# First attention of a two-layer vision transformer: closing steps and weight splits at other bursts, and the guard's branch between two scores

## The chip, the cores and the metric

The kernel is one program on one core of a Trainium2 chip. The metric is device time in microseconds (us), the median of several executions. The engines are PE (TensorE, matrix products), VectorE (DVE), ScalarE (ACT), GpSimd (POOL) and SyncE (SP, which issues DMAs); each works its own instruction list in order, and semaphores tie them together.

## The reference

Eight images of 32 x 32 tokens pass a tokeniser and two layers, each of attention and a mixture of experts. The part that the change touches is the first attention, with softmax over 1024 keys in 8 heads of 16, and its closing:

```python
h = tok(x)                                # (8, 1024, 128)
xn = layernorm(h)
Q, K, V = (xn @ Wq.T + bq, xn @ Wk.T + bk, xn @ Wv.T + bv)   # 8 heads of 16
attn = softmax(Q K^T / 4);  context = attn V
out = context @ Wo.T + bo + xn
out = (out - mean) / sqrt(var + 1e-5) * gamma + beta
h = h + out                               # first residual
h = h + moe_0(layernorm(h), ...)          # 2 of 8 experts for an image
h = h + attn_1(layernorm(h), ...);  h = h + moe_1(layernorm(h), ...)   # 2 of 8 for a token
```

(In the reference the layer's heads come from a plain reshape, so each head of an image holds 128 tokens' worth of rows, spread over the eight column groups.)

## The kernel before

`embed_and_attend` does the first attention. A **batch** is one image; there are eight. A batch has 64 **units**: four head pairs (HP) of 16 units. For a unit PE makes scores (`scores`, L826) of 128 keys against 512 queries for both heads of the pair into one of three psS buffers, ScalarE takes the exponential of all 128 x 1024 (L741) into one of four probs buffers, and PE multiplies them by the values into psO (`weigh`, L838). Two units are a **burst**; a batch has 32 bursts, numbered m, and eight of them make a pair. In burst m PE waits for the exponential of unit 2m + 1, issues the scores of units 2m + 3 and 2m + 4, at a pair's first burst the projection of an earlier pair (`project`, L391), then `weigh` for units 2m and 2m + 1, and then a step of the next batch's embedding.

At a **pair change** (between bursts 7 and 8, 15 and 16, 23 and 24, 31 and 0) VectorE must transpose psO out (`out_of_psum`, L1015, in the last burst of a pair) before PE may begin the next pair's first value product. After it come `add_input` (L397), which frees psA for PE's next step, and `divide` (L1019 to L1025).

Between these, three kinds of work hang on the burst numbers.

- **Steps of the next batch** (`STEPS`): E embeds, T transposes, q and k project, N takes norms for the guard, v projects; each for two halves (0, 1). VectorE reads each result (`embed_read`) and works it on (`embed_rest`); GpSimd squares q and k (L671). N waits on PE for the square of k of its half.
- **Closing steps** (`finish`), for half 0 and half 1 of a batch's tokens: add_bias (L435, then moments), normal (L105), moments, second (L105, L448), score (L450, L452). GpSimd has a part in three of them: a root (L402) after add_bias and after moments, and after normal the **stream** (L410, L412, L414), which updates the residual and which moments waits for. `UPPER` holds those done in the batch after, `LOWER` those in the same batch. The order of the table sets VectorE's and GpSimd's order alike.
- **Weight splits** (`SPLIT`): VectorE splits one raw expert weight tile in two (L1031, L1033), GpSimd stores the result (L710) and loads the next raw tile (L705). A split waits for its tile's load and for the store before.

The **guard** bounds the scores. At burst 24 VectorE branches on the flag `unsafe` (`guard`), and on PE `rescue` (L812) reads the same flag at burst 25; with this input neither branch is entered. `drain` on an engine waits until its earlier writes are done.

The last batch (`more` false) has no steps of a next one; it has the gating of the experts (`GATES`, `POOLED`, `PE_TILES`) and its own splits.

## Time and profile before

| | |
|---|---|
| median of 3 runs | 1405.86 us (1405.33 to 1407.46) |
| profiled execution | 1408.95 us |
| its span in the trace | 1407.1 us |
| PE busy | 1187.5 us (84%) |
| ScalarE busy | 995.0 us (71%) |
| VectorE busy | 934.7 us (66%) |
| GpSimd busy | 564.4 us (40%) |
| first attention, first to last exponential | from 56.6 to 624.5 us |

The busy shares are means over four stages with different limits. What matters here is the first 630 us, and in them which engine waits for which. A wait in square brackets at the end of a timeline row is the engine's idle time just before it.

### The profile page before, as it was taken

Reading aid. Unit: us, or ns where it says so; the run is one execution under the profiler, and the core shown is the slowest. Engines: PE = TensorE matmul, PEld = TensorE weight load, DVE = VectorE, ACT = ScalarE, POOL = GpSimd, SP = SyncE. Lnnn points to the kernel's source line nnn. Section 1 sums busy time; section 2 is a strip of 40 time slices with the busy share of each in tenths; the row PEclk is TensorE's granted clock in tenths of the full one; section 3 lists DMA queues with packets and bytes.
Section 4 is the critical chain, followed back from the end, with each engine's and each line's share of the span. In section 5 each row is a group of like instructions: output and inputs, shape, how many; then the busy total and the mean of one; then the engine's idle time right before and its main releaser. Section 6 shows DMA issues by size and latency. Waiting matters only on the chain. (4 is left out here: it accounts for less than half of the span.)

```text
span 1407.1 us, 26982 instructions
## 1 busy us (share of the span) xinstructions
PE 1187.5 (84%) x9386; PEld 795.1 (57%) x9386; DVE 934.7 (66%) x2612; ACT 995.0 (71%) x1348; POOL 564.4 (40%) x546
## 2 busy tenths in 40 slices
PE   3599999999999999889989996888872899999940
PEld 2244444444444444447768874777762688888830
DVE  4255868686868686758978884677662466666625
ACT  0288888888888888858868984454520799999930
POOL 3413333333333333210201000077777177777660
PEclk9599999999999999979999997889875899999975
DMA  3655565555555555223211300011115577777609
GB/s 86 119 129 146 120 157 130 147 130 148 139 138 137 138 135 139 84 71 124 88 61 61 119 2 8 1 49 47 50 47 174 181 242 237 241 245 244 234 24 358
DMA packets 93163, 180.57 MB, mean 128 GB/s; under 512 B 15597, under 2 KB 64200, under 8 KB 84960
## 3 DMA queue, kind: packets, MB, share of 16 engines
q1 hardware_dynamic: 72832, 129.18, 32.8%
q0 software_dynamic: 17344, 42.68, 9.4%
q10 hardware_dynamic: 2848, 6.95, 1.7%
q8 instruction: 76, 1.25, 0.4%
q14 instruction: 63, 0.52, 0.1%
HBM read 116.96 MB, written 63.12 MB: 128 GB/s over the span
## 5 line engine op out<-in xcount | busy, mean ns | idle before, releaser
L741 ACT ACTIVATE a_probs<-a_psS 128x1024 f32<-128x1024 f32 x512 | 484.0, 1034 | 91.5 <-PE a_psS L826 58.2
L838 PE MATMUL a_psO<-a_probs,a_v 128*32 128x256 f32 x4096 | 282.1, 394 | 17.3 <-DVE a_o_t L1015 16.9
L1252 DVE TENSOR_TENSOR f_g_lo<-f_g,f_g_hi 128x512 fp32r<-128x512 f32 x284 | 195.1, 689 | 121.1 <-ACT f_g L1159 120.1
L2044 POOL DMA_INDIRECT result<-f_out,f_idx x156 | 182.7, 1171 | 92.5 <-issue 61.0
L838 PEld LDWEIGHTS a_psO<-a_probs,a_v 128*32 128x32 f32 x4096 | 108.5, 111 | 154.0 <-issue 88.9
L1636 POOL DMA_INDIRECT queue<-all_row,all_idx x128 | 126.0, 984 | 38.5 <-issue 37.8
L826 PE MATMUL a_psS<-ag_qs,ag_ks 50*128 50x512 f32 x512 | 97.4, 457 | 15.7 <-DMA ag_qs<-a_gparts 8.5
L826 PE MATMUL a_psS<-a_qs,a_ks 50*128 50x512 f32 x512 | 96.8, 454 | 7.8 <-issue 3.4
L402 POOL TENSOR_TENSOR ag_rs_f<-ag_veps_f,all_half 128x4 f32<-128x4 f32 x32 | 34.1, 1066 | 124.4 <-DVE ag_veps_f L99 124.4
L1422 POOL TENSOR_TENSOR ah_rs<-ah_veps,all_half 128x4 f32<-128x4 f32 x16 | 18.5, 1156 | 154.3 <-DVE ah_veps L1435 154.2
L826 PEld LDWEIGHTS a_psS<-ag_qs,ag_ks 50*128 50x128 f32 x512 | 39.9, 191 | 63.4 <-issue 31.6
L826 PEld LDWEIGHTS a_psS<-a_qs,a_ks 50*128 50x128 f32 x512 | 39.3, 189 | 54.7 <-ACT a_probs L741 37.5
L1166 ACT ACTIVATE f_x_hi<-f_psX 128x512 fp32r<-128x512 f32 x55 | 33.1, 602 | 43.2 <-PE f_psX L1191 43.2
L710 POOL DMA_DIRECT2D experts<-a_split x32 | 19.7, 615 | 108.6 <-DVE a_split L1033 108.6
L1156 ACT ACTIVATE f_g_hi<-f_psH,all_w 128x512 fp32r<-128x512 f32 x76 | 53.1, 699 | 10.1 <-PE f_psH L72 9.5
L1156 ACT ACTIVATE f_g_hi<-f_psH,ag_qs 128x512 fp32r<-128x512 f32 x72 | 50.3, 699 | 12.3 <-PE f_psH L72 11.6
L1156 ACT ACTIVATE f_g_hi<-f_psH,f_w 128x512 fp32r<-128x512 f32 x64 | 44.6, 697 | 18.9 <-PE f_psH L72 17.9
L1156 ACT ACTIVATE f_g_hi<-f_psH,ag_ks 128x512 fp32r<-128x512 f32 x72 | 51.0, 708 | 7.9 <-PE f_psH L72 7.5
L1159 ACT ACTIVATE f_g<-f_psH,all_w 128x512 f32<-128x512 f32 x76 | 53.1, 699 | 0.0
L1159 ACT ACTIVATE f_g<-f_psH,ag_ks 128x512 f32<-128x512 f32 x72 | 51.0, 709 | 0.0
L1159 ACT ACTIVATE f_g<-f_psH,ag_qs 128x512 f32<-128x512 f32 x72 | 50.3, 699 | 0.0
L1191 PE MATMUL f_psX<-all_ident,all_rows 128*128 128x128 f32 x156 | 24.4, 281 | 28.7 <-DMA all_rows<-queue 26.3
(368 smaller groups left out, 2878.8 us busy)
## 6 DMA issues: line engine op xcount, KB each, us to landing
all_w<-experts SPq DMA_DIRECT2D x19, 1026.5 KB, 5.5
experts<-a_split POOLq DMA_DIRECT2D x32, 512.0 KB, 4.8
ag_qs<-experts SPq DMA_DIRECT2D x14, 1026.5 KB, 5.3
ag_ks<-experts SPq DMA_DIRECT2D x14, 1026.5 KB, 5.2
all_rows<-queue SPq DMA_DIRECT2D x39, 260.0 KB, 5.1
f_w<-experts SPq DMA_DIRECT2D x8, 1026.5 KB, 5.5
qparts<-a_parts SPq DMA_DIRECT2D x16, 512.0 KB, 4.5
kparts<-a_parts SPq DMA_DIRECT2D x14, 512.0 KB, 3.1
```

The lines of the kernel that those rows point to most:

```text
L402: self.nc.gpsimd.tensor_tensor(self.rs_f[:, :], self.veps_f[:, :], half[:, 0:TPC], ALU.pow).then_inc(self.root_f, 1)
L710: pool.dma_start(experts[stage][e, :, 2 * layer * HID:2 * (layer + 1) * HID], split[:, :, :].rearrange("p a h -> p (a h)").bitcast(F32)).t ...
L741: nc.scalar.activation(probs[u % NPR][:, :], psS[score_buffer(u)][:, :, :].rearrange("p a n -> p (a n)"), ACT.Exp).then_inc(exp_done, 1)
L826: last = nc.tensor.matmul(psS[score_buffer(u)][:, p, :], ks[par][64 * p:64 * p + KG, kt, hp * P:(hp + 1) * P], queries(par, hp, p, a), sta ...
L838: last = nc.tensor.matmul(psO[32 * g:32 * g + 32, a * HALF:(a + 1) * HALF], v[par][:, 2 * hp + p, kt, :], probs[u % NPR][:, cols:cols + HA ...
L1156: nc.scalar.activation(g_hi[i][:, n, :], psH[n][:, :], ACT.Gelu, bias=bias(m, n))
L1159: nc.scalar.activation(g[:, n, :], psH[n][:, :], ACT.Gelu, bias=bias(m, n)).then_inc(g_done, 1)
L1166: nc.scalar.activation(x_hi[j % 2][:, :], psX[:, :], ACT.Copy).then_inc(hi_done, 1)
L1191: last = nc.tensor.transpose(psX[:, i * P:(i + 1) * P], rows(m)[:, i, 0:D], ident[:, :])
L1252: nc.vector.tensor_tensor(g_lo[i][:, n, :], g[:, n, :], g_hi[i][:, n, :].bitcast(F32), ALU.subtract).then_inc(lo_done, 1)
L1636: pool.indirect_dma_start(queue, bass.IndirectOffsetOnAxis(ap=idx[n % NROW][:, k, t:t + 1], axis=0), row[n % NROW][:, k, t, :], None).then ...
L2044: pool.indirect_dma_start(result, bass.IndirectOffsetOnAxis(ap=idx[i][:, j:j + 1], axis=0), out[i][:, j, :], None, bounds_check=2 * B * S ...
```

## The change

It changes numbers in three tables and one position in PE's code.

- Splits of batches 0 to 6 go from bursts 7, 15, 22, 27 to 10, 14, 22, 28.
- Of the closing steps, moments 0 goes from burst 2 of the next batch to burst 30 of the same (`LOWER`, and for the last batch, which `KEEP` leaves out, it stays where it was, behind this phase). Second 0 goes from 4 to 2, score 0 from 6 to 4, add_bias 1 from 10 to 15, normal 1 from 12 to 18, moments 1 from 18 to 20, score 1 from 25 to 26, add_bias 0 from 26 to 25, normal 0 from 28 to 27. Second 1 stays at 23.
- `rescue` on PE stands between the scores of units 53 and 54 instead of ahead of both. Its spare score buffer is then one (`FREE`), not two, which changes only code inside the branch.

```diff
-    SPLIT = [{7: 0, 15: 1, 22: 2, 27: 3}] * (B - 1) + [{5: 0, 12: 1, 16: 2, 21: 3}]
+    SPLIT = [{10: 0, 14: 1, 22: 2, 28: 3}] * (B - 1) + [{5: 0, 12: 1, 16: 2, 21: 3}]
...
-    FREE = (score_buffer(2 * RESCUE), score_buffer(2 * RESCUE + 1))
-    UPPER = {2: ("moments", 0), 4: ("second", 0), 6: ("score", 0), 10: ("add_bias", 1), 12: ("normal", 1), 18: ("moments", 1), 23: ("second", 1),
-             25: ("score", 1)}
-    LOWER = {26: ("add_bias", 0), 28: ("normal", 0)}
+    FREE = score_buffer(2 * RESCUE + 4)
+    UPPER = {2: ("second", 0), 4: ("score", 0), 15: ("add_bias", 1), 18: ("normal", 1), 20: ("moments", 1), 23: ("second", 1), 26: ("score", 1)}
+    LOWER = {25: ("add_bias", 0), 27: ("normal", 0), 30: ("moments", 0)}
+    KEEP = (25, 27)
...
-                    if m in LOWER:
+                    if m in LOWER and (more or m in KEEP):
...
-                    if more and m == RESCUE:
-                        rescue(b + 1, 1 - par, uses.next())
-                        uses.count -= 1
                     for u in (2 * m + 3, 2 * m + 4):
                         if u < UNITS or more:
                             scores(b, par, u)
+                        if more and u == 2 * RESCUE + 3:
+                            rescue(b + 1, 1 - par, uses.next())
+                            uses.count -= 1
```

GpSimd in a steady batch, from the square of q of the first half at burst 9 to the split's store at burst 22, before:

```order
L671 TENSOR_TENSOR a_qsq<-a_qf 128x512
L402 TENSOR_TENSOR ag_rs_f<-ag_veps_f,all_half 128x4
L671 TENSOR_TENSOR a_ksq<-a_kf 128x512
L410 TENSOR_TENSOR ag_res<-ag_res,ag_brow 128x512
L412 TENSOR_TENSOR ag_res<-ag_res,ag_brow 128x512
L414 TENSOR_TENSOR all_H<-all_H,ag_res 128x512
L710 DMA experts<-a_split 128x1024
L705 DMA a_raw<-w 128x512
L671 TENSOR_TENSOR a_qsq<-a_qf 128x512
L402 TENSOR_TENSOR ag_rs_f<-ag_veps_f,all_half 128x4
L671 TENSOR_TENSOR a_ksq<-a_kf 128x512
L710 DMA experts<-a_split 128x1024
```

and with the change, from the same square of q to the second half's square of k at burst 19:

```order
L671 TENSOR_TENSOR a_qsq<-a_qf 128x512
L710 DMA experts<-a_split 128x1024
L705 DMA a_raw<-w 128x4x128
L671 TENSOR_TENSOR a_ksq<-a_kf 128x512
L710 DMA experts<-a_split 128x1024
L705 DMA a_raw<-w 128x512
L402 TENSOR_TENSOR ag_rs_f<-ag_veps_f,all_half 128x4
L671 TENSOR_TENSOR a_qsq<-a_qf 128x512
L410 TENSOR_TENSOR ag_res<-ag_res,ag_brow 128x512
L412 TENSOR_TENSOR ag_res<-ag_res,ag_brow 128x512
L414 TENSOR_TENSOR all_H<-all_H,ag_res 128x512
L671 TENSOR_TENSOR a_ksq<-a_kf 128x512
```

The stream (L410 to L414) stood behind the first half's square of k; now it stands between the second half's squares of q and k.

VectorE in a steady batch around the change at burst 15, from the read of the transposed second half (T 1, burst 13) to the read of q of that half (burst 17), before:

```order
L105 TENSOR_SCALAR ag_res<-ag_res,ag_mv_f,ag_rs_f 128x128 x4
L912 COPY a_nT<-a_psA 128x512
L940 CAST a_nT_hi<-a_nT 128x512
L942 TENSOR_TENSOR a_nT_lo<-a_nT,a_nT_hi 128x512
L1015 STREAM_TRANSPOSE a_o_t<-a_psO 128x512
L1031 CAST a_split<-a_raw 128x512
L1033 TENSOR_TENSOR a_split<-a_raw,a_split 128x512
L397 TENSOR_TENSOR ag_res<-a_psA,ag_n 128x256
```

and with the change:

```order
L912 COPY a_nT<-a_psA 128x512
L940 CAST a_nT_hi<-a_nT 128x512
L942 TENSOR_TENSOR a_nT_lo<-a_nT,a_nT_hi 128x512
L1031 CAST a_split<-a_raw 128x512
L1033 TENSOR_TENSOR a_split<-a_raw,a_split 128x512
L1015 STREAM_TRANSPOSE a_o_t<-a_psO 128x512
L435 TENSOR_TENSOR ag_res<-ag_res,ag_brow 128x512
L94 BN_STATS ag_stat_f<-ag_res 128x6 x4
L97 BN_AGGR ag_mv_f<-ag_stat_f 128x2 x4
L99 TENSOR_SCALAR ag_veps_f<-ag_mv_f 128x4
L397 TENSOR_TENSOR ag_res<-a_psA,ag_n 128x256
```

Normal 1 (L105) is gone from the place in front, the split (L1031, L1033) stands ahead of the transpose instead of behind it, and add_bias 1 (L435 to L99) stands between the transpose and add_input (L397).

PE at burst 25, the first of the places where it stands:

```order
 L391 MATMUL a_psA<-ag_w_raw,ag_ctxT 128x128 x2
 L838 MATMUL a_psO<-a_probs,a_v 32x256 x8
+L826 MATMUL a_psS<-ag_qs,ag_ks 128x512 x2
 L812 TENSOR_LOAD a_unsafe
 L812 ISA x2
```

One of the burst's two scores (two products) now stands ahead of the load of the flag; the other follows the branch.

## Rows read from the trace of the kernel before

**Rows 1.** The page's part 5: line, engine, group, count; busy, mean ns; idle before, by releaser.

```profile
L741 ACT ACTIVATE a_probs<-a_psS 128x1024 f32<-128x1024 f32 x512 | 484.0, 1034 | 91.5 <-PE a_psS L826 58.2
```

**Rows 2.** Timeline of ScalarE, batch 4: start, us, what, count, idle before.

```profile
361.59 2.86 ACT L741 ACTIVATE a_probs<-a_psS 128x1024 f32<-128x1024 f32 x3 [1.66 <-PE a_psO L838]
...
379.46 2.86 ACT L741 ACTIVATE a_probs<-a_psS 128x1024 f32<-128x1024 f32 x3 [1.73 <-PE a_psO L838]
...
397.91 5.61 ACT L741 ACTIVATE a_probs<-a_psS 128x1024 f32<-128x1024 f32 x6 [1.17 <-PE a_psS L826]
...
413.51 2.85 ACT L741 ACTIVATE a_probs<-a_psS 128x1024 f32<-128x1024 f32 x3 [0.29 <-PE a_psO L838]
```

**Rows 3.** Timeline of PE, batch 4.

```profile
357.03 1.07 PE L838 MATMUL a_psO<-a_probs,a_v 128*32 128x256 f32 x16
...
374.82 1.07 PE L838 MATMUL a_psO<-a_probs,a_v 128*32 128x256 f32 x16
...
378.69 1.07 PE L838 MATMUL a_psO<-a_probs,a_v 128*32 128x256 f32 x16 [1.37 <-DVE a_o_t L1015]
...
389.89 0.38 PE L772 MATMUL a_psA<-a_ksq,a_pieces 128*32 128x512 bf16 x1
...
397.37 0.73 PE L826 MATMUL a_psS<-ag_qs,ag_ks 50*128 50x512 f32 x4 [1.34 <-issue]
```

**Rows 4.** Timeline of VectorE, batch 4, bursts 2 to 18.

```profile
351.19 0.87 DVE L94 BATCH_NORM_STATS2 ag_stat_f<-all_H 128x6 f32<-128x128 f32 x4
...
360.07 0.71 DVE L1015 STREAM_TRANSPOSE a_o_t<-a_psO 128x512 f32<-128x512 f32 x1
...
372.62 1.88 DVE L105 TENSOR_SCALAR ag_res<-ag_res,ag_mv_f,ag_rs_f 128x128 f32<-128x128 f32 x4
...
377.94 0.70 DVE L1015 STREAM_TRANSPOSE a_o_t<-a_psO 128x512 f32<-128x512 f32 x1
...
380.11 0.42 DVE L397 TENSOR_TENSOR ag_res<-a_psA,ag_n 128x256 f32<-128x256 f32 x1
...
382.35 0.75 DVE L918 TENSOR_SCALAR a_qf<-a_psA,a_bcol 128x512 f32<-128x512 f32 x1 [0.19 <-PE a_psA L72]
...
384.47 0.87 DVE L94 BATCH_NORM_STATS2 ag_stat_f<-all_H 128x6 f32<-128x128 f32 x4
```

**Rows 5.** Timeline of GpSimd, batch 4, the stream and the squares.

```profile
372.60 1.04 POOL L671 TENSOR_TENSOR a_ksq<-a_kf 128x512 bf16<-128x512 f32 x1 [1.16 <-DVE a_parts L951]
374.58 1.29 POOL L410 TENSOR_TENSOR ag_res<-ag_res,ag_brow 128x512 f32<-128x512 f32 x1 [0.93 <-DVE ag_res L105]
...
377.60 1.53 POOL L414 TENSOR_TENSOR all_H<-all_H,ag_res 128x512 f32<-128x512 f32 x1
...
388.69 1.04 POOL L671 TENSOR_TENSOR a_ksq<-a_kf 128x512 bf16<-128x512 f32 x1 [1.53 <-DVE a_parts L951]
```

**Rows 6.** Timeline of VectorE, batch 4, bursts 26 to 31.

```profile
401.47 0.69 DVE L435 TENSOR_TENSOR ag_res<-ag_res,ag_brow 128x512 f32<-128x512 f32 x1
...
403.91 0.69 DVE L926 TENSOR_TENSOR a_v<-a_psA,ag_brow 128x512 f32<-128x512 f32 x1
...
405.80 1.12 DVE L105 TENSOR_SCALAR ag_res<-ag_res,ag_mv_f,ag_rs_f 128x128 f32<-128x128 f32 x4
...
411.45 0.72 DVE L1015 STREAM_TRANSPOSE a_o_t<-a_psO 128x512 f32<-128x512 f32 x1 [2.67 <-PE a_psO L838]
```

**Rows 7.** Loads of the raw weight tile, 300 to 420 us: issue to landing.

```profile
DMA to landing us min/median/max: 4.4/6.4/11.1
```

**Rows 8.** Timeline of ScalarE in the last batch.

```profile
562.61 0.24 ACT L221 ACTIVATE ag_e_sc<-ag_sc 128x48 f32<-128x48 f32 x1 [1.48 <-DVE ag_sc L281]
...
589.37 2.85 ACT L741 ACTIVATE a_probs<-a_psS 128x1024 f32<-128x1024 f32 x3 [1.88 <-PE a_psO L838]
```

**Rows 9.** Timeline of VectorE in the last batch.

```profile
625.66 1.11 DVE L105 TENSOR_SCALAR ag_res<-ag_res,ag_mv_f,ag_rs_f 128x128 f32<-128x128 f32 x4 [1.15 <-POOL ag_rs_f L402]
```

**Rows 10.** Two us behind a pair change of batch 1: engines' busy time, PEclk, DMA.

```profile
152.00:154.00 2.00, 2.00 (x16) 0.77 (x18) 1.89 (x6) 1.08 (x2) 0.99 (x2) 0.50 0.64 244
```

More of the change, by code:

```diff
@@ L796, in maximum @@
                         rows, cols = slice(64 * p, 64 * p + KQ), slice(hp * P, (hp + 1) * P)
-                        pe.wait_ge(pre_max, j * T + (b * (T * KT) + h + 1))
+                        pe.wait_ge(pre_max, j * T + (b * (T * KT) + h + 2))
                         for a in range(2):
-                            last = nc.tensor.matmul(psS[FREE[h % 2]][:, a, :], stage[rows, cols], ks[par][rows, 4 * a:4 * a + 4, cols],
+                            last = nc.tensor.matmul(psS[FREE][:, a, :], stage[rows, cols], ks[par][rows, 4 * a:4 * a + 4, cols],
                                                     start=True, stop=True)
@@ L981, in maximum @@
                         dve.sem_inc(waited, 1)
-                        nc.vector.tensor_reduce(negmax[:, h % 2, bass.ds(j, 1), h // 2], psS[FREE[h % 2]][:, :, :].rearrange("p a n -> p (a n)"),
+                        nc.vector.tensor_reduce(negmax[:, h % 2, bass.ds(j, 1), h // 2], psS[FREE][:, :, :].rearrange("p a n -> p (a n)"),
                                                 AX, ALU.max, negate=True).then_inc(pre_max, 1)
@@ L1074, in batch @@
                         shared.finish(dve, part, b - 1, half_, H, mean1, rstd1, score1)
-                    if m in LOWER:
+                    if m in LOWER and (more or m in KEEP):
                         part, half_ = LOWER[m]
```

## The prediction

> **What bounds the kernel now.** I read the page's costliest groups first, then the waits of ScalarE, then one steady batch row by row on every engine. The attention phase runs 512 exponentials one behind the other; ScalarE is busy 484.0 us with them and idle 91.5 us in front of them [rows 1]. Only that idle time can be won. All times below are of batch 4, the fifth of eight.
>
> In that batch ScalarE waits 1.66 us at unit 20 and 1.73 us at unit 36, behind the pair changes at bursts 8 and 16, but only 0.29 us behind the one at burst 0 [rows 2]. The first two come from VectorE. At burst 7 the last value product starts at 357.03 and takes 1.07, so it is done at 358.10 [rows 3]; the transpose that empties psO starts at 360.07, 1.97 late, since VectorE is still at earlier steps [rows 4]. At burst 15 the product is done at 374.82 + 1.07 = 375.89 and the transpose starts at 377.94, 2.05 late [rows 3, 4]; PE then stands 1.37 before the new pair's first product [rows 3]. At burst 31 VectorE waits for PE instead (2.67 idle ahead of the transpose at 411.45) [rows 6], and the change costs the 0.29. A transpose 1.97 late costs 1.66 - 0.29 = 1.37, so about 0.6 us of lateness is hidden (by the projection that PE does there). The fourth idle place is the guard's branch: PE idle 1.34, ScalarE 1.17 [rows 2, 3].
>
> **Burst 7.** Moments 0 leaves burst 2. It costs what add_bias costs without its addition: 403.91 - 401.47 - 0.77 = 1.67 us [rows 6]. The score moves from 6 to 4, the split from 7 to 10: order alone. The transpose moves from 360.07 to 358.4, 0.3 late, which is hidden. Gain 1.37.
>
> **Burst 15.** Add_bias 1 and normal 1 leave the bursts in front of it (2.44 and, with its block, 1.88) and two splits of some 1.2 us each come in. GpSimd's three-part update (stream) leaves too; in the old order the transposed tile's split waited it out. VectorE then has time to spare, if the second weight tile is in. The transpose falls to 375.89 - 1.37 = 374.5 and the gain is 1.73 - 0.29 = 1.44. Together 2.81 per batch by burst 17.
>
> **Burst 21, where I expect it to be given back.** In the new order GpSimd does the stream between the squares of q and k of the second half. PE's norm step N 1 at burst 21 waits for the square of k, which so far lay ahead of nothing but a root. The chain, from the transpose at 374.55 on: 0.64 for it, 2.44 for add_bias 1 (now between the transpose and add_input), 382.35 - 380.11 - 0.19 = 2.05 for add_input and division, so q 1 is read at 379.7 [rows 4, 6]. Its parts take 384.47 - 382.35 = 2.12, to 381.8, and GpSimd squares them. Normal 1 goes in beside that square; the same pair lay together at 372.60, and normal 1 took 1.88 there against 1.12 alone [rows 4 to 6]. So it ends at 383.65. The stream took 377.60 + 1.53 - 374.58 = 4.55, so it ends at 388.3, and the square of k, 1.04, at 389.4 [rows 5]. N 1 started at 389.89 before [rows 3]; with the pair changes won it would be due at 389.89 - 2.81 = 387.1, and can now start at 389.5. PE stands 2.4 us, its next scores are late by that, and ScalarE has about nothing in hand here. What is left of 2.81 is 0.4.
>
> Normal 1's time hangs on the block. The Trainium skill (SBUF — State Buffer, on its engine ports) says that VectorE in a two-port mode or with two SBUF inputs and a GpSimd instruction hold the shared port pair exclusively, and the loser waits the whole instruction. By that rule the block returns beside the q square, as the row shows; without it the sum would be 0.76 better per batch.
>
> **Burst 31.** The sum of add_bias 0 and score 1 is what it was, so v 0 is read at 403.91 less some 0.2. Normal 0 now follows at once, to 405.5 (1.12); the stream ends at 410.1, moments 0 can only then run, to 411.8. The transpose stood at 411.45 [rows 6]; it would now be due at about 410.8. It is late by a full us, 0.6 of it hidden. What burst 25 and the remainder of burst 21 won (0.3 + 0.4) is all but gone: the new batch starts 0.1 earlier, measured against the old. The split pushed behind it waits for GpSimd's instructions too; nothing needs it soon.
>
> **The branch.** PE still runs it in line; only one score, 0.33 us of PE, now lies beside it, and ScalarE gets unit 53 on time but waits for unit 54 instead. Worth 0.3 on PE's chain, not 1.17, because the steps v 0 and v 1 behind it keep PE the limit. If nothing of it overlaps it is 0, if ScalarE were the limit it would be 0.9. I take 0.3 (nearest to the row of PE).
>
> **The weight tile.** It is loaded behind the split at burst 10 (old clock 368.4) and wanted by the split at burst 14, from 373.4 on. Landings ran from 4.4 to 11.1, median 6.4 [rows 7]; the 4.4 fell into quiet DMA, as most of this one does. I take 5.2, so 0.2 us late, which delays the whole chain to burst 21. Bounds: 4.4 costs nothing, 6.4 costs 1.4.
>
> So a steady batch ends with -0.1 + 0.2 = +0.1; for batches 1 to 6 that is 0.6. Batch 0 has no closing steps of a batch before; I take 0.
>
> **The last batch** keeps its splits and has no k square, so there the moves are free. (a) ScalarE waits 1.48 at unit 10 for the shift [rows 8]; ahead of the shift moments 0 goes (1.67) and second 0 comes (1.12 for an instruction group like normal 0, and 0.2 for a copy), and the division there no longer meets a stream, whose instructions last 1.3 and block for half of that on average: 1.67 - 1.3 + 0.7 = 1.1. (b) The change at burst 16 costs 1.88 [rows 8]; with add_bias 1 and normal 1 out of the way 1.88 - 0.29 = 1.6. (c) At the end add_bias 0 stands a burst earlier and normal 0 no longer waits for its root, 1.15 before [rows 9]; 0.9 of it reaches the phase's end. Together 3.6.
>
> **The sum.** 3.6 - 0.6 = 3.0 us. The profiled execution took 1408.95; so 1405.95 in it. The runs' median is 1405.86, 3.09 below the profiled one, so 1402.9. A measurement here tells 0.2%, 2.8 us, from no change; 3.0 lies on that edge. Own range of this case: each steady batch by 0.4 either way (2.4 us), the last by 1: 1399.5 to 1406.
>
> **Rivals.**
> - *The square of k is not late* (chance 0.15). If add_bias or the division run sooner or PE has slack at burst 21, the 2.81 stays in part. Each us that N 1 comes earlier is worth 6 us; half of the wait gone gives 1402.9 - 7 = 1396, all of it 1389. For it: the order itself was laid out to free the pair changes, and both transposes have room. Against: four GpSimd instructions stand in line, with rows for each.
> - *The weight tile is late* (0.12, the slower side). At a landing of 6.4 each of six batches loses 1.2 more than I took: 1402.9 + 7 = 1410. It decides from a landing of about 6.2, where the kernel becomes slower by over 0.2%. For it: k's parts are stored and loaded again just then. Against: 4.4 in the same burst range before.
> - *The clock* (0.08). The granted clock was 0.50, that is 1.2 GHz, for 2 us behind the pair change of batch 1 [rows 10], after PE had stood still at it. The new stand at burst 21 is longer. A dip costs about 1.3 (the exponentials come at 1.5 us there instead of 0.94); in four batches more than before 5 us: 1408. With fewer stands at pair changes it may as well fall away.
> - *The last batch gives nothing* (0.15): its gains are eaten by the summing of the pooled tiles, which now runs under the stream and feeds burst 21. Then 1402.9 + 2.5 = 1405.4, no change.
>
> My forecast has 0.5. Its range lies half on either side of 1403.05, the edge, with more on the faster side. Faster: 0.15 + 0.31 + 0.03 = 0.49. Slower: 0.09 of the weight tile, 0.03 of the clock, 0.01 of the rest: 0.13. Same: 0.38. The range leaves out a tenth at each end: the full gain of the first rival below, the late tile above: 1394 to 1409.
>
> **What would show it.** In the trace after: ScalarE's waits at units 20 and 36 at 0.3 in each steady batch; a new wait of some 2 us at unit 47, put down to scores, with N 1 waiting for the square of k; GpSimd's stream between the two squares; the wait at unit 4 grown from 0.29 to 0.7 or so; that at 53 gone and one of about 1 at 54; VectorE waiting for stream_done at burst 30; steady batches still 70 us long. In the last batch the 1.88 and most of the 1.48 gone. I am wrong if unit 47 has no wait, if unit 36 still has one of over 1, or if batches shorten by more than 0.5 us.

## The result, and the profile after

| | before | after |
|---|---|---|
| median of the runs on one chip | 1405.46 us (20 runs) | 1413.8 us (20 runs, 1410.31 to 1419.44) |
| ratio after to before, 95% interval | | 1.006 [1.0045, 1.0074] |
| profiled execution, its span | 1408.95 us, 1407.1 us | 1411.72 us, 1409.9 us |
| start of unit 4, batches 1 and 7 | 132.83 and 555.52 us | 124.19 and 559.79 us |
| a steady batch, a sixth of that | 70.45 us | 72.60 us |
| start of unit 4 of batch 7 to last exponential | 69.0 us | 66.4 us |

The changed kernel is slower by 0.6%, some 8 us; the forecast was 1402.9. In the profiled executions a steady batch is 2.15 us longer instead of 0.1, and the last one 2.6 shorter instead of 3.6. The spans differ by only 2.8 us, because the profiled execution of the kernel before lost time at its start: its first exponential stands at 56.6 instead of 52.1, ahead of everything that the change touches, and from there to unit 4 of batch 1 it took 76.2 us instead of 72.1. (Two other kernels whose batch 0 is that of before, in experiments 3 and 9, took 71.8 and 72.1.)

The answer to [rows 1], the page's part 5: the exponentials are as long as before, and the idle time looks hardly more, 92.1 us against 91.5. That sum hides the loss. Batch 0 has 19.1 us of it before (8.12 in front of the first exponential) and 9.2 after (2.48 there); the six steady batches have 58.6 and 68.8.

```profile
L741 ACT ACTIVATE a_probs<-a_psS 128x1024 f32<-128x1024 f32 x512 | 485.3, 1033 | 92.1 <-PE a_psS L826 64.5
```

Timeline of ScalarE, batch 5 of after, which answers to [rows 2] (units 20, 36, 47, 48, 49, 50, 52 and then unit 4 of the next batch):

```profile
433.22 2.86 ACT L741 ACTIVATE a_probs<-a_psS 128x1024 f32<-128x1024 f32 x3 [0.29 <-PE a_psO L838]
...
449.70 2.86 ACT L741 ACTIVATE a_probs<-a_psS 128x1024 f32<-128x1024 f32 x3 [0.29 <-PE a_psO L838]
...
463.88 1.02 ACT L741 ACTIVATE a_probs<-a_psS 128x1024 f32<-128x1024 f32 x1 [2.81 <-PE a_psS L826]
465.20 1.02 ACT L741 ACTIVATE a_probs<-a_psS 128x1024 f32<-128x1024 f32 x1 [0.29 <-PE a_psO L838]
466.71 1.02 ACT L741 ACTIVATE a_probs<-a_psS 128x1024 f32<-128x1024 f32 x1 [0.48 <-PE a_psS L826]
467.99 1.94 ACT L741 ACTIVATE a_probs<-a_psS 128x1024 f32<-128x1024 f32 x2 [0.26 <-PE a_psO L838]
470.28 6.63 ACT L741 ACTIVATE a_probs<-a_psS 128x1024 f32<-128x1024 f32 x7 [0.36 <-PE a_psO L838]
...
488.11 2.85 ACT L741 ACTIVATE a_probs<-a_psS 128x1024 f32<-128x1024 f32 x3 [1.49 <-PE a_psO L838]
```

Both pair changes are won: 0.29 at units 20 and 36. A wait of 2.81 has come in at unit 47. Three small ones follow it; the exponentials start 1.3 to 1.5 us apart there. And unit 4 waits 1.49 instead of 0.29. The mean over batches 1 to 6 makes a ledger of ScalarE's waits (of 0.15 us and more), in us per batch:

| units | before | after | forecast of the difference |
|---|---|---|---|
| 20 and 36 | 3.31 | 0.58 | -2.81 |
| 47 | 0 | 3.12 | +2.4 |
| 48 to 52 | 0.29 | 1.58 | 0 |
| 53 to 58 | 1.03 | 0 | (-0.3 on PE) |
| 4 | 0.29 | 1.60 | +0.4 |
| others | 4.86 | 4.59 | 0 |
| all | 9.78 | 11.47 | |

The rest of the 2.15 is in no printed wait: exponentials in a row overlap a little (seven take 6.63 above), and one that stands alone takes 1.02.

The chain behind unit 47, in three timelines of the same batch. VectorE (answers to [rows 4]), the transpose of burst 15, add_input, normal 1, and moments 1:

```profile
447.64 0.72 DVE L1015 STREAM_TRANSPOSE a_o_t<-a_psO 128x512 f32<-128x512 f32 x1 [0.27 <-PE a_psO L838]
...
455.04 1.88 DVE L105 TENSOR_SCALAR ag_res<-ag_res,ag_mv_f,ag_rs_f 128x128 f32<-128x128 f32 x4
...
461.91 0.87 DVE L94 BATCH_NORM_STATS2 ag_stat_f<-all_H 128x6 f32<-128x128 f32 x4 [1.80 <-POOL all_H L414]
```

GpSimd (answers to [rows 5]), the stream between the two squares:

```profile
455.02 1.04 POOL L671 TENSOR_TENSOR a_qsq<-a_qf 128x512 bf16<-128x512 f32 x1 [3.12 <-DVE a_parts L951]
456.99 1.29 POOL L410 TENSOR_TENSOR ag_res<-ag_res,ag_brow 128x512 f32<-128x512 f32 x1 [0.93 <-DVE ag_res L105]
458.93 1.55 POOL L412 TENSOR_TENSOR ag_res<-ag_res,ag_brow 128x512 f32<-128x512 f32 x1 [0.65 <-issue]
460.62 1.26 POOL L414 TENSOR_TENSOR all_H<-all_H,ag_res 128x512 f32<-128x512 f32 x1
461.84 1.04 POOL L671 TENSOR_TENSOR a_ksq<-a_kf 128x512 bf16<-128x512 f32 x1
```

PE (answers to [rows 3]), N 1 and the burst behind it:

```profile
463.02 0.38 PE L772 MATMUL a_psA<-a_qsq,a_pieces 128*32 128x512 bf16 x1 [2.69 <-POOL a_ksq L671]
...
464.00 1.93 PE L838 MATMUL a_psO<-a_probs,a_v 128*32 128x256 f32 x16
465.87 1.22 PE L826 MATMUL a_psS<-a_qs,a_ks 50*128 50x512 f32 x4
```

N 1 starts 463.02 - 447.64 = 15.38 us behind the transpose; the forecast's chain has 389.5 - 374.55 = 14.95. PE stands (is idle and waits) for 2.69 us. What the forecast does not have is in the next row: the 16 value products take 1.93 where [rows 3] has 1.07, and the four score products 1.22 instead of 0.73. Windows of 2 us say why; the granted clock is the figure behind the five engines' busy times:

```profile
462.00:464.00 2.00, 0.98 (x6) 0.42 (x6) 1.77 (x11) 0.12 (x1) 1.31 (x2) 1.00 0.88 263
464.00:466.00 2.00, 2.00 (x20) 0.75 (x18) 1.60 (x8) 1.71 (x2) 0.59 (x1) 0.51 1.08 181
466.00:468.00 2.00, 2.00 (x20) 0.83 (x20) 0.81 (x2) 1.26 (x3) 0.81 (x2) 0.63 1.13 168
468.00:470.00 2.00, 2.00 (x28) 1.13 (x24) 1.54 (x5) 1.93 (x2) 0.59 (x1) 1.00 1.15 168
```

After the stand PE works at 0.51, that is 1.2 GHz, for some 3 us, is busy all of that time and still gives ScalarE a tile only every 1.3 to 1.5 us. The answer to [rows 10] is this in every one of the six steady batches; in those of the kernel before, the clock fell in two (at 151 and 519 us).

At burst 31 VectorE's moments 0 waits for the stream, and the transpose is late (its wait for PE in [rows 6] is gone):

```profile
485.02 0.87 DVE L94 BATCH_NORM_STATS2 ag_stat_f<-all_H 128x6 f32<-128x128 f32 x4 [2.05 <-POOL all_H L414]
...
486.58 0.71 DVE L1015 STREAM_TRANSPOSE a_o_t<-a_psO 128x512 f32<-128x512 f32 x1
```

In the last batch the 1.88 of [rows 8] is 0.29, and nothing is left of the 1.48 in front of the exponential of the gating. But PE stands long at the sum of the pooled tiles, half a pair behind, and unit 47 waits 4.61:

```profile
606.76 1.30 PE L246 MATMUL a_psA<-ag_ones,ag_n 128*128 128x1 f32 x8 [3.28 <-DVEq L317]
```

The phase's end, which answers to [rows 9]: ScalarE's first instruction behind the last exponential, before and after.

```profile
633.51 0.60 ACT L1166 ACTIVATE f_x_hi<-f_psX 128x512 fp32r<-128x512 f32 x1 [7.84 <-PE f_psX L1191]
```

```profile
635.41 0.60 ACT L1166 ACTIVATE f_x_hi<-f_psX 128x512 fp32r<-128x512 f32 x1 [8.11 <-issue]
```

The last exponential starts at 624.5 and at 626.2, so that stretch takes 9.0 us before and 9.2 after: nothing is won there.

### The profile page after: what moved, and what is told of

It is laid out like the page before. It is cut to its first block and busy times, and to the rows that moved or that the text cites. A ratio compares the mean times of both kernels' runs of the same rounds, so it can differ in the third digit from the quotient of the medians.

```text
span 1409.9 us, 26982 instructions
## 1 busy us (share of the span) xinstructions
PE 1192.5 (85%) x9386; PEld 796.0 (56%) x9386; DVE 929.1 (66%) x2612; ACT 996.4 (71%) x1348; POOL 565.2 (40%) x546
## 5 line engine op out<-in xcount | busy, mean ns | idle before, releaser
L741 ACT ACTIVATE a_probs<-a_psS 128x1024 f32<-128x1024 f32 x512 | 485.3, 1033 | 92.1 <-PE a_psS L826 64.5
L2044 POOL DMA_INDIRECT result<-f_out,f_idx x156 | 183.1, 1174 | 92.1 <-issue 61.3
L671 POOL TENSOR_TENSOR a_qsq<-a_qf 128x512 bf16<-128x512 f32 x16 | 17.4, 1090 | 102.5 <-DVE a_parts L951 102.5
```

The source lines that it names most:

```text
L741: nc.scalar.activation(probs[u % NPR][:, :], psS[score_buffer(u)][:, :, :].rearrange("p a n -> p (a n)"), ACT.Exp).then_inc(exp_done, 1)
L2044: pool.indirect_dma_start(result, bass.IndirectOffsetOnAxis(ap=idx[i][:, j:j + 1], axis=0), out[i][:, j, :], None, bounds_check=2 * B * S ...
```

## The experiments

Each ratio is to the kernel before on the same chip; kernels are compared with each other by these ratios, since the chips differ. "A batch" is again a sixth of the time from unit 4 of batch 1 to unit 4 of batch 7, in one profiled execution. It scatters by itself: two kernels with the steady batches of before have 70.45 and 71.28 in theirs. In the first the granted clock fell twice in these batches, in the second five times, four of them at pair changes.

### 1. N 1 two bursts later

```diff
-             20: ("N", 0), 21: ("N", 1), 27: ("v", 0), 29: ("v", 1)}
+             20: ("N", 0), 23: ("N", 1), 27: ("v", 0), 29: ("v", 1)}
```

> The changed kernel with one step moved: PE's second norm product, N 1, stands at burst 23 instead of 21, so the square of k has two bursts more. Theory A (the loss is PE's stand of 2.7 us at burst 21, and the half clock that follows it): the wait at unit 47 (2.8 to 3.7 us in batches 1 to 6) and the clock's fall at bursts 22 and 23 (1.5 us a batch) go; of the 4 us some 1.5 come back as a longer wait at burst 31, so 2 to 2.5 us for each of six batches: 12 to 15 us under the changed kernel's 1413.8, a ratio to before of 0.995 to 0.998. Theory B (the loss is at burst 31, moments 0 behind its stream): the wait at unit 47 goes but the one at unit 4 grows by as much, the time stays within 3 us of the changed kernel's, ratio 1.004 to 1.006.

Measured: 1415.01 us, 1.009 [1.0062, 1.0119]; a batch 71.64. The wait at unit 47 is gone, and ones of 1.9 to 3.2 at unit 52 and 0.9 to 3.1 at unit 4 stand in its place; the clock still falls four times in the steady batches. Timeline of PE: the projection at the pair change waits for N 1's result to be read, which VectorE does late.

```profile
468.56 0.71 PE L391 MATMUL a_psA<-ag_w_raw,ag_ctxT 128*128 128x128 f32 x4 [1.49 <-DVE a_norms L921]
```

Neither theory foresaw that. N 1 as such is no cure: the stand has moved.

### 2. Seven products that nobody reads, ahead of N 1's wait

```diff
                 elif kind == "N":
+                    if b and ch:
+                        for i in range(7):
+                            nc.tensor.matmul(ps, wq_lo[:, :], nT_hi[ch][:, :], start=True, stop=True)
                     pe.wait_ge(sq_done, 2 * n)
```

> The changed kernel, with seven products of 512 columns that nothing reads put on PE ahead of N 1's wait for the square of k (2.3 us of work in a stand of 2.7); the result is unchanged. It parts the stand's own length from the clock. If the half clock behind the stand comes from PE's idleness in it, the granted clock stays at full through bursts 22 and 23, and 1.5 us a batch come back: 8 to 9 us under the changed kernel, ratio 1.000. If the clock falls for another reason (DMA, or what the steps are), nothing comes back: ratio 1.005 to 1.007.

Measured: 1402.76 us, 0.9984 [0.9964, 1.0004]; a batch 70.48. The kernel does more and N 1 starts no earlier (15.32 us behind the transpose, 15.38 without the products), yet by the ratios it is 11 us faster than the changed kernel, and the intervals lie apart. Timeline of PE, batch 5, and one window:

```profile
452.82 1.90 PE L772 MATMUL a_psA<-a_nT_hi,a_wq_lo 128*128 128x512 f32 x7
455.52 0.39 PE L775 MATMUL a_psA<-a_qsq,a_pieces 128*32 128x512 bf16 x1 [0.80 <-POOL a_ksq L671]
...
456.51 1.07 PE L841 MATMUL a_psO<-a_probs,a_v 128*32 128x256 f32 x16
```

```profile
456.00:458.00 2.00, 2.00 (x24) 0.86 (x24) 1.60 (x8) 1.61 (x2) 1.02 (x1) 1.00 1.11 166
```

PE's idle time is 0.80 instead of 2.69, the value products take 1.07, and the clock stays at 1.00 in all six steady batches. ScalarE still waits 2.82 at unit 47 (mean of six), but 0 instead of 1.16 at units 48 to 51 and 0.98 instead of 1.60 at unit 4. So the stand by itself gives back what the two pair changes won, and the clock behind it is what makes the change slower than the kernel before. (The products aren't free: in batch 0, where there is no stand to fill, unit 47 now waits 1.86.)

### 3. The branch alone, in the kernel before

```diff
-                    if more and m == RESCUE:
-                        rescue(b + 1, 1 - par, uses.next())
-                        uses.count -= 1
                     for u in (2 * m + 3, 2 * m + 4):
                         if u < UNITS or more:
                             scores(b, par, u)
+                        if more and u == 2 * RESCUE + 3:
+                            rescue(b + 1, 1 - par, uses.next())
+                            uses.count -= 1
```

(with `FREE` as in the change)

> The kernel before with the third part of the change alone: the guard's branch on PE between the two scores of burst 25. By my prediction's term 0.3 us a batch, 2 us in all: ratio 0.9985. By the trace of the changed kernel, where the load of the flag takes 0.30 us instead of 1.1 to 1.2 and PE is idle 0.3 instead of 1.34, some 1 us a batch: 6 to 7 us, ratio 0.995. ScalarE's wait at unit 53 (0.66 to 1.28) gone, at unit 54 under 0.7.

Measured: 1406.11 us, 1.0013 [0.9992, 1.0034]; a batch 70.46, against 70.45. The wait at unit 53 is gone, 0.46 to 1.39 stand at unit 54. No gain shows: the 0.3 a batch would be 0.9985, just outside the interval. Nor did the load of the flag become short by its place: its median is 768 ns here, 870 in the kernel before and 304 in the changed one.

### 4. Moments 0 at burst 0 of the next batch, in the changed kernel

```diff
-    UPPER = {2: ("second", 0), ...
-    LOWER = {25: ("add_bias", 0), 27: ("normal", 0), 30: ("moments", 0)}
+    UPPER = {0: ("moments", 0), 2: ("second", 0), ...
+    LOWER = {25: ("add_bias", 0), 27: ("normal", 0)}
```

> The changed kernel with moments 0 not at burst 30 but at burst 0 of the next batch, behind the transpose and the division, where VectorE is idle for 2 us before the embedding's read. Theory B: the wait at unit 4 falls from 1.5 to 2.0 us to 0.29, 1.2 to 1.7 us a batch for seven changes, 8 to 12 us: ratio 0.998 to 1.000. Theory A: the same wait goes, since it is there, but the stand at burst 21 stays as it is (2.7), and with it its half clock: the time is 1405 to 1408.

Measured: 1408.54 us, 1.0023 [1.0004, 1.0042]. Unit 4 is back at 0.29 in every steady batch, so the late transpose of burst 31 was moments 0's. By the ratios some 5 us of the loss go with it, though the intervals all but touch. The clock still falls in all six steady batches.

### 5. Both repairs

The added lines of experiment 2 and the tables of experiment 4 together, in the changed kernel.

> The changed kernel with both repairs: seven unread products ahead of the wait of N 1 for the square of k (the square itself, and N 1's start, stay as late as they are), and moments 0 at burst 0 of the next batch instead of burst 30. Theory (the lower granted clock behind the stand at unit 47 and the late transpose at burst 31 each cost time of their own): no dip, unit 47 still waits 2.7 to 3.3 us, unit 4 is back at 0.3; steady batches of 69.6 to 69.9 us against 70.5 with the fill alone, so some 4 us less than that one: 1398 to 1400, ratio to before 0.994 to 0.997. Rival (the wait at unit 4 is only what ScalarE is ahead of PE, so its loss comes back at the next wait of PE): as with the fill alone, 1401 to 1404, ratio 0.997 to 1.000.

Measured: 1401.46 us, 0.9963 [0.9945, 0.9981]; a batch 69.77, as the theory had it; the clock stays at 1.00 in the steady batches, unit 47 waits 2.82 and unit 4 0.29. Against experiment 2 that is 0.7 a batch in the traces, 1.3 us by the medians and 3 us by the ratios, whose intervals overlap: the repair of burst 31 is seen in the traces, and its size in the whole kernel is not settled.

### 6. Half 1's closing steps back in their places

```diff
-    UPPER = {..., 15: ("add_bias", 1), 18: ("normal", 1), 20: ("moments", 1), ...}
+    UPPER = {..., 10: ("add_bias", 1), 12: ("normal", 1), 18: ("moments", 1), ...}
```

> The changed kernel with half 1's closing steps where they were before (add_bias 1 at burst 10, normal 1 at 12, moments 1 at 18); splits, half 0's steps and the branch stay changed. Theory (the stream between the squares of q and k of half 2 makes the stand at unit 47, and the clock's fall follows from it): no wait over 0.8 at unit 47, granted clock 1.00 there; unit 36 waits 1.0 to 1.8 again, since normal 1 and the split at burst 14 stand ahead of the transpose; unit 4 still 1.5 to 2.0; steady batches of 69.8 to 70.5 us, total 1403 to 1408, ratio 0.998 to 1.002. Rival (the clock falls because of the splits or of burst 31): dips stay and the batches are 71.5 to 72.5 us, total over 1411.

Measured: 1415.28 us, 1.0073 [1.0045, 1.01]; a batch 72.85. Unit 47 no longer waits, and nothing is gained: unit 36 waits 3.25 to 4.1. Timelines of VectorE and of PE, batch 5:

```profile
447.91 1.88 DVE L105 TENSOR_SCALAR ag_res<-ag_res,ag_mv_f,ag_rs_f 128x128 f32<-128x128 f32 x4
...
453.03 1.59 DVE L1033 TENSOR_TENSOR a_split<-a_raw,a_split 128x512 fp32r<-128x512 f32 x1
454.55 0.70 DVE L1015 STREAM_TRANSPOSE a_o_t<-a_psO 128x512 f32<-128x512 f32 x1
```

```profile
455.30 1.93 PE L838 MATMUL a_psO<-a_probs,a_v 128*32 128x256 f32 x16 [3.29 <-DVE a_o_t L1015]
```

The split that the change put ahead of the transpose now meets the stream (1.59 instead of 0.69), and the transpose starts after both. My expectation had the place right and the size at less than half. The granted clock falls behind this stand too, in all six steady batches (PE idle for 2.89 to 3.29 us): the value products take 1.93 again. So the rival is right in the total and half right in the cause. The split ahead of the transpose is part of what makes the stand, and the clock falls behind the stand, wherever it is. The last batch went the other way: from unit 4 to the last exponential 61.7 us, against 69.0 before and 66.4 in the changed kernel, with the clock at 1.00 throughout and no product added.

### 7. The kernel before with the stream ahead of both squares

```diff
-    UPPER = {2: ("moments", 0), 4: ("second", 0), 6: ("score", 0), 10: ("add_bias", 1), 12: ("normal", 1), 18: ("moments", 1), 23: ("second", 1),
-             25: ("score", 1)}
-    LOWER = {26: ("add_bias", 0), 28: ("normal", 0)}
+    UPPER = {0: ("moments", 0), 2: ("second", 0), 4: ("score", 0), 10: ("add_bias", 1), 16: ("normal", 1), 18: ("moments", 1), 23: ("second", 1), 26: ("score", 1)}
+    LOWER = {25: ("add_bias", 0), 27: ("normal", 0)}
```

(and the last split of a batch at 28 instead of 27)

> The kernel before with another order: moments 0 at burst 0, second 0 at 2, score 0 at 4, add_bias 1 at 10, normal 1 at 16, moments 1 at 18, score 1 at 26, add_bias 0 at 25, normal 0 at 27, last split at 28; other splits and the branch as before. The stream now stands ahead of both squares of the second half and behind the transpose of burst 15. Theory (what the change lost is the stream between the squares, and burst 31): units 20 and 36 wait 0.3 to 0.6, unit 47 under 0.8, unit 4 0.3; if the 2.8 us of the two pair changes stay, steady batches are 67.5 to 68.5 us and the total is 1388 to 1396, ratio 0.987 to 0.993. Rival (PE is the limit of the batch, so that what is won at a pair change comes back as waits at the steps and at unit 53): batches of 69.5 to 70.3, total 1401 to 1406, ratio 0.997 to 1.000.

Measured: 1435.9 us, 1.0205 [1.0172, 1.0239]; a batch 76.15. Units 20, 36 and 4 wait 0.3 as expected, but unit 45 waits 7.3 to 8.2. Timeline of GpSimd, batch 5 (issue of the raw tile's load, then the stream), and the landing of that load:

```profile
462.98 0.55 POOL L704 DMA_DIRECT2D a_raw<-W  x1
465.32 1.28 POOL L410 TENSOR_TENSOR ag_res<-ag_res,ag_brow 128x512 f32<-128x512 f32 x1 [1.79 <-DVE ag_res L105]
473.05 1.26 POOL L412 TENSOR_TENSOR ag_res<-ag_res,ag_brow 128x512 f32<-128x512 f32 x1 [6.44 <-issue]
```

```profile
a_raw<-W POOLq DMA_DIRECT2D x1, 256.0 KB, 9.7
```

Between L410 and L412 stands a drain. It ended at about 473, and the load landed at 462.98 + 9.7 = 472.7: the drain also waited for GpSimd's own load in flight. Where no load is under way the gap is 0.65 or less (rows above). The kernel before has the same wait in half 0's stream: in batches 0 to 6 the gap is 2.6 to 3.6 us, and L412 starts 0.5 to 0.8 behind the landing of the load issued just ahead of the stream. Timeline of GpSimd, batch 4 of before:

```profile
406.60 0.55 POOL L705 DMA_DIRECT2D a_raw<-W  x1
407.17 1.29 POOL L410 TENSOR_TENSOR ag_res<-ag_res,ag_brow 128x512 f32<-128x512 f32 x1
411.80 1.28 POOL L412 TENSOR_TENSOR ag_res<-ag_res,ag_brow 128x512 f32<-128x512 f32 x1 [3.34 <-issue]
```

Moments 1 at burst 18 waited 8.09 for the stream, with k 1's read behind it. Both theories missed it.

### 8. The change in the last batch alone

```diff
     LOWER = {26: ("add_bias", 0), 28: ("normal", 0)}
+    UPPER_LAST = {2: ("second", 0), 4: ("score", 0), 15: ("add_bias", 1), 18: ("normal", 1), 20: ("moments", 1), 23: ("second", 1), 26: ("score", 1)}
+    LOWER_LAST = {25: ("add_bias", 0), 27: ("normal", 0)}
...
+                    if m == 30 and b == B - 2:
+                        finish("moments", b, 0)
```

> The kernel before in batches 0 to 6 (but moments 0 of the seventh batch at its burst 30), and the closing steps of the change in the last batch alone. The prediction's term: 3.6 us gained, ratio 0.9974, total about 1402.3. Theory from the trace after: unit 36 gains 1.6 and unit 10 some 0.5 to 1, but moments 1 at burst 20 waits for the stream and the summing of the pooled tiles behind it holds PE for some 3 us, and the end gives nothing: between 1 us gained and 2 us lost, ratio 0.999 to 1.0015.

Measured: 1409.29 us, 1.0028 [1.0007, 1.0049]. It doesn't isolate the last batch: moments 0 at burst 30 of the seventh stands only two bursts behind normal 0 there, waits 6.13 for the stream, and unit 4 of the last batch waits 5.2. From there on the trace has 67.0 us to the last exponential, 69.0 before: the wait at unit 36 is won (0.29), those at units 45 and 47 are 2.27 as before, so the theory's 3 us at the pooled tiles did not come here. The term of 3.6 stays unmeasured by a run's time.

### 9 and 10. Score products issued twice in the last batch

```diff
-                for p in range(2):
+                for p in (0, 0, 1) if b == B - 1 and 16 <= u < 56 and u % 2 else (0, 1):
```

> The kernel before, with one of the two score products of every second unit from 16 to 55 of the last batch issued twice (the same values into the same buffer, 20 products more); nothing else. Theory (in the last batch PE has no steps of a next batch, its idleness lets the granted clock fall to half for some 12 us, and PE at half speed makes the exponentials come slower): the clock stays at 1.00 from unit 16 to unit 55 of the last batch, the waits of 2.26 at units 45 and 47 shrink to under 1, and 3 to 6 us go: 1400 to 1403, ratio 0.996 to 0.998. Rival (the length of the last batch is set by the gating's chain on VectorE and by the pooled sums, the clock only follows): same waits, ratio 0.999 to 1.002.

Measured, in the kernel before: 1402.58 us, 0.9973 [0.9954, 0.9991]. A window of 2 us in the last batch of before:

```profile
604.00:606.00 2.00, 2.00 (x19) 0.92 (x11) 0.00 (x0) 1.34 (x2) 0.00 (x0) 0.50 0.00 0
```

and of this kernel:

```profile
604.00:606.00 2.00, 2.00 (x31) 1.10 (x27) 0.52 (x3) 2.00 (x3) 0.00 (x0) 1.00 0.04 8
```

Before, the clock is at 0.50 from 598 to 610; with 20 products more it is 1.00 throughout, and from unit 4 to the last exponential it takes 65.1 us instead of 69.0. Added work made the kernel before faster.

The same line in the kernel of experiment 5:

> The changed kernel with the seven unread products ahead of N 1's wait, with moments 0 at burst 0, and with the repeated score products in the last batch. If the two repairs of the clock add up: 4 us less than without the repeated products, 1396 to 1399, ratio 0.992 to 0.995. If the last batch is set by the wait of the pooled sums (4.9 at unit 47) and not by the clock: the same as without them, 1401, ratio 0.996 to 0.997.

Measured: 1402.21 us, 0.9976 [0.9956, 0.9996], no gain over experiment 5. In its last batch the clock still falls to 0.50 twice, at 558 to 562 and behind the wait of 3.24 at unit 47.

### 11 and 12. The stream behind the square of k

```diff
-    UPPER = {2: ("second", 0), 4: ("score", 0), 15: ("add_bias", 1), 18: ("normal", 1), 20: ("moments", 1), ...
-    LOWER = {25: ("add_bias", 0), 27: ("normal", 0), 30: ("moments", 0)}
+    UPPER = {0: ("moments", 0), 2: ("second", 0), 4: ("score", 0), 15: ("add_bias", 1), 19: ("normal", 1), 22: ("moments", 1), ...
+    LOWER = {25: ("add_bias", 0), 27: ("normal", 0)}
```

(and half 1 of the last batch as before)

> The changed kernel with moments 0 at burst 0, normal 1 at burst 19 (so that the stream stands behind the square of k, not in front of it), moments 1 at 22, and the last batch's half 1 as before (10, 12, 18). No product is added. Theory (the stand of PE at unit 47 comes from the stream between the squares and takes the clock with it): N 1 waits under 0.5, no wait over 1 at unit 47, clock 1.00, units 20, 36 and 4 at 0.3; steady batches of 68.0 to 69.2 us, total 1392 to 1398, ratio 0.990 to 0.995. Rival one (PE is the limit, so the batch has 69.7 us as with the fill and moments 0 together): 1399 to 1402. Rival two (moments 1 at burst 22 waits for the stream and makes the transpose of burst 23 late): unit 52 waits 1.5 to 3, dips, batches over 71, total over 1408.

Measured: 1409.38 us, 1.0026 [1.0005, 1.0047]; a batch 71.83. The second rival: moments 1 waits for the stream and the transpose of burst 23 stands behind it. Timeline of VectorE, batch 5:

```profile
460.96 1.87 DVE L105 TENSOR_SCALAR ag_res<-ag_res,ag_mv_f,ag_rs_f 128x128 f32<-128x128 f32 x4
462.93 0.68 DVE L922 TENSOR_REDUCE a_norms<-a_psA 64x1 f32<-64x512 f32 x1
...
467.56 0.88 DVE L94 BATCH_NORM_STATS2 ag_stat_f<-all_H 128x6 f32<-128x128 f32 x4 [1.23 <-POOL all_H L414]
...
470.22 0.71 DVE L1016 STREAM_TRANSPOSE a_o_t<-a_psO 128x512 f32<-128x512 f32 x1
```

Unit 52 waits 2.5 to 3.0 for it and the clock falls. Unit 47 still waits 1.46: normal 1, held by the square of k to 1.87, stands ahead of the read of N 0, for which N 1 waits.

The same kernel with the repeated score products of experiment 9:

> The kernel above (stream behind the square of k) with the repeated score products in the last batch. If its last batch has a stretch at half clock: 3 to 5 us less than without them, 1388 to 1394, ratio 0.988 to 0.992. If the last batch keeps its clock anyway: the same as without them.

Measured: 1405.48 us, 1.0008 [0.998, 1.0035]; some 4 us less, the difference that was expected (the intervals overlap). The total of 1388 to 1394 was not reached, since the kernel it builds on had not reached its own.

### 13 and 14. The closing steps spread out

Each of the two waits just read gets room: normal 1 behind the read of N 1, moments 1 behind the transpose.

```diff
+    SPLIT = [{10: 0, 14: 1, 22: 2, 29: 3}] * (B - 1) + ...
+    UPPER = {0: ("moments", 0), 2: ("second", 0), 4: ("score", 0), 15: ("add_bias", 1), 21: ("normal", 1), 24: ("moments", 1), 25: ("second", 1), 27: ("score", 1)}
+    LOWER = {26: ("add_bias", 0), 28: ("normal", 0)}
```

(and half 1 of the last batch as before)

> The changed kernel with the closing steps at other bursts: moments 0 at 0, second 0 at 2, score 0 at 4, add_bias 1 at 15, normal 1 at 21 (behind the read of N 1), moments 1 at 24 (behind the transpose of burst 23), second 1 at 25, add_bias 0 at 26, score 1 at 27, normal 0 at 28, last split at 29; the last batch with half 1 as before (10, 12, 18, 23, 25). No product added or left out. Theory (the change's loss is the two places where VectorE or PE wait for the stream, and the clock behind them; PE is not the limit): no wait over 0.7 at units 4, 20, 36, 47 and 52, clock 1.00 in the steady batches, each of 66.8 to 68.5 us, total 1388 to 1396, ratio 0.988 to 0.993. Rival (PE limits a batch to the 69.7 that the fill with moments 0 at burst 0 has, waits only move): 1400 to 1403, ratio 0.996 to 0.999. Second rival (VectorE between bursts 24 and 31 now has too much, v 0 or v 1 or the transpose of burst 31 is late): waits of over 1 at units 57 to 63 or at unit 4, total over 1403.

Measured: 1394.1 us, 0.9905 [0.9878, 0.9931]; a batch 68.55. Timeline of ScalarE, batch 5 (units 36, 43, 52, and 4 of the next):

```profile
435.96 2.86 ACT L742 ACTIVATE a_probs<-a_psS 128x1024 f32<-128x1024 f32 x3 [0.29 <-PE a_psO L839]
...
443.53 8.43 ACT L742 ACTIVATE a_probs<-a_psS 128x1024 f32<-128x1024 f32 x9 [0.45 <-PE a_psS L827]
453.61 6.52 ACT L742 ACTIVATE a_probs<-a_psS 128x1024 f32<-128x1024 f32 x7 [1.65 <-PE a_psO L839]
...
470.31 2.85 ACT L742 ACTIVATE a_probs<-a_psS 128x1024 f32<-128x1024 f32 x3 [0.29 <-PE a_psO L839]
```

Nine exponentials run without a gap where the changed kernel stands at unit 47. PE is not what held a batch at 69.7, and the gains at the pair changes can be kept. One wait of 1.65 is left, at unit 52, and unit 20 waits up to 0.86 in some batches.

And with the repeated score products:

> The kernel above with the repeated score products in the last batch, 20 of them. As in the runs before (2.4 and 3.9 us less with them): 2 to 4 us under e_spread, clock 1.00 through the last batch, ratio 0.986 to 0.991. If the last batch keeps its clock anyway: the same as e_spread, or 1 us more.

Measured: 1388.93 us, 0.9888 [0.9864, 0.9912]; from unit 4 of the last batch to the last exponential 65.3 us instead of 73.5. (Without the products the clock was at 0.5 from 550 to 560 and from 588 to 600 us in that batch.) This is the fastest kernel of the study, 16 us under the kernel before; its interval and that of the kernel without the products overlap.

### 15. The third split at burst 18, with the repeated products

```diff
-    SPLIT = [{10: 0, 14: 1, 22: 2, 29: 3}] * (B - 1) + ...
+    SPLIT = [{10: 0, 14: 1, 18: 2, 29: 3}] * (B - 1) + ...
```

> The spread order with the repeated score products, and its third split at burst 18 instead of 22. In the spread order the transpose of burst 23 starts behind normal 1 (1.11), and a split of 0.42 and 1.61 (the 1.61 beside the stream), and unit 52 waits 1.65. At burst 18 VectorE is idle for 1.89. Theory (the late transpose sets that wait): unit 52 at 0.3 to 0.5, steady batches of 66.8 to 67.3 us instead of 68.2, six of them: 6 to 8 us less, 1381 to 1383, ratio 0.983 to 0.985. Rivals: the raw tile, loaded at 430.1 + 0.6, lands behind 438 and holds k 1's read (unit 47 waits 0.5 to 1.5, a gain of 0 to 3); or PE is the limit (unit 52 gains, units 54 or 63 lose the same: 1388 to 1390).

Measured: 1404.44 us, 1.0004 [0.9975, 1.0033]; a batch 70.31. Unit 52 waits 0.29, but the gain is gone: the first rival came, and larger. Timeline of VectorE, batch 5:

```profile
448.90 0.43 DVE L1032 CAST a_split<-a_raw 128x512 fp32r<-128x512 f32 x1 [3.09 <-DMA a_raw<-W]
```

The load was issued at 439.12 and wanted 6.7 us later; it was in only at 448.9. K 1's read waits behind it, unit 45 waits 1.2 to 1.9 in five of six batches, and unit 63 waits 1.6 to 1.8 instead of 0.7 to 1.1 (why is not settled). The clock stays at 1.00 in these batches, so it has no part in this loss.

## Why the prediction was wrong, point by point

- **Bursts 7 and 15: right.** Gain 2.81 forecast, 2.73 in the mean of six batches; experiment 13 shows that it is there to keep.
- **Burst 21: right in place and mechanism, a little small.** Stand 2.4 forecast, 2.69 in batch 5 and up to 3.06 in others, and 3.12 of wait on ScalarE in the mean (2.82 where the clock is held). The row of normal 1 beside the square is the 1.88 that was put in. The Trainium skill (SBUF — State Buffer, on its engine ports) has the same: the loser of the shared port pair waits the whole instruction. The trace agrees: of the four instructions in the row at 455.04 the first lasts 1.10 us, to just behind the end of the square, and the others 0.33.
- **The clock: the step that failed.** The prediction left the granted clock out of its sum, and had it only as a rival of 0.08, with 1.3 us a dip "in four batches more than before", 5 us in all. The count was right: the clock fell in all six steady batches, against two of them before. The price right behind the stand was right too: units 48 to 52 wait 1.58 instead of 0.29. Wrong were the zero in the sum and the price as a whole: with the clock held in the same kernel (experiment 2) a batch is 72.60 - 70.48 = 2.12 us shorter and the kernel 11 us faster, since units 47 and 4 wait less as well. I had the stand of 1.37 with value products of 1.07 behind it, full speed [rows 3], and one case of 0.50 [rows 10], and did not ask what a stand twice as long as the first would do each time. The Trainium skill (TensorE: Matmul & The Clock Gate, on its oscillation in real kernels) tells of a kernel whose PE waits in every step of its loop and drops to half clock each time; the trace of the changed kernel agrees, once a batch.
- **The rest of the sum, with the clock held.** A batch then takes 70.48 (before 70.45, forecast +0.1) and the kernel 1402.76 us (forecast 1402.9). That they meet so closely is in part luck. The terms at unit 47, at unit 4 and of the branch are each 0.3 to 0.4 worse than forecast. Against that, the 70.45 of before holds two falls of the clock (in the two batches with one ScalarE waits 10.0 and 10.9 us, in the other four 9.3 to 9.6), which the kernel with the fill doesn't have.
- **Burst 31: place right, size too small.** Wait at unit 4: 0.4 more forecast, 0.69 more with the fill, 1.31 more in the changed kernel.
- **The branch: 0.3 forecast, nothing measured** (experiment 3), the lower of the bounds given.
- **The weight tile: 0.2 forecast.** VectorE waited 0.63 for it in batch 1 and not at all in the other five steady batches. Experiment 15, where a tile was wanted 6.7 us behind its issue and took 9.8, shows that the rival was real, only at another burst.
- **The last batch: 3.6 forecast, 2.6 in the traces up to the last exponential.** The parts (a) and (b) came, with the whole 1.48 and with 1.59. Some 0.4 of that was lost at the sum of the pooled tiles, which stood 3.28 and took the clock with it, as the fourth rival had it in part. Part (c), 0.9 at the phase's end, did not come: 9.2 us there against 9.0. Not isolated by an experiment.

Shown by runs: that the change's loss is the granted clock's (experiment 2), that moments 0 makes unit 4 late (4), and that the gain of the pair changes can be kept once the steps that wait for the stream, and those behind it, have room (13, 14). That the stream's place between the squares makes the stand at unit 47 is read in the traces; experiment 11 moved the stream, and the wait there fell from 3.12 to 1.46. Only read in traces: the split of the last batch's gain.

## What to carry to other kernels

A new stand of PE is priced twice: its own length, and the products behind it at the lower clock, if the rows show the clock falling behind a stand of that length; then look for the next place where the later PE meets an in-order engine. Steps that wait for a slow neighbour belong behind the instruction that another engine is waiting for, with bursts of distance, and a step is moved only after reading what it stands in front of on each queue. Where PE must be idle anyway, a few unread products are a cheap test of whether the clock is the cost, and sometimes the cure. A sum of idle time over the whole kernel can hide such a loss; a ledger by unit shows it.

## What the runs showed of the hardware

- PE idle for 2.69 us and then at 0.51 of full clock for some 3 us; with 0.80 idle in the same place it stayed at 1.00. In the steady batches of the changed kernel and of experiments 6 and 11 PE was idle once a batch for 2.17 to 3.29 us, and the clock fell each of these 18 times; behind the 0.80 to 0.90 of experiment 2 it fell in none of six. Behind the 0.86 to 1.37 at the pair changes of the kernel before it fell in 2 of 12, and with the same steady batches in experiment 9 in 4 of 12.
- In a stretch where PE was not stopped for long but had less to do (last batch of before), the clock stayed at 0.50 for 12 us, and 20 products more kept it at 1.00: 0.9973 of the time.
- A drain on GpSimd waited until a load that GpSimd had issued was in: 6.44 us, to 473.05, the load landing at 472.7. In the kernel before the same drain took 2.6 to 3.6 us with a load in flight and 0.32 without.
- Landings of the same 256 KB tile: 9.7 us beside the parts' transfers (experiment 7), against a median of 6.4 [rows 7].
- PE's load of the guard's flag takes an uneven time: 483/870/1222 ns (least, median, greatest of 8) before, 299/304/853 after, and 488/768/1608 with the branch at its new place in the kernel before (experiment 3). Why is open.
